# Query pass of a two-layer kernel: the output projection and the router's columns as one 136-column product, the logits read before the residual's addition

## The reference

```python
# third block, per token (q is already in its second-order form)
out = einsum(q, kv_state) / maximum(einsum(q, k_sum), 1e-5)     # 8 heads of 16
y   = out.reshape(b, n, 128) @ w_out
x   = x + layernorm(y)
# fourth block
flat = layernorm(x)
probs = softmax(flat @ Wr)            # 8 experts, the 2 best are chosen
output = sum over the chosen e of weight_e * ((silu(flat @ Wg[e]) * (flat @ Wu[e])) @ Wd[e])
x = x + layernorm(output)
```

## Time and profile before

| | |
|---|---|
| median of 3 runs | 718.79 us |
| lowest and highest run | 717.28 and 718.93 us |
| span of the profiled execution, first to last instruction | 713.3 us |
| mean granted TensorE clock over the span | 0.847 of 2.4 GHz |
| TensorE busy | 518.2 us (73%) |
| VectorE busy | 426.9 us (60%) |
| ScalarE busy | 332.8 us (47%) |

### The profile page before, as it was taken

One profiled execution on the slowest core, in us unless ns is written; L12 is line 12 of the kernel. 1 busy time (PEld: TensorE's weight loads), 2 busy tenths in 40 slices (PEclk: granted clock), 3 DMA queues, 4 the chain that ended last, 5 costly groups with the idle time before them and its releaser, 6 DMA issues.

```text
span 713.3 us, 13599 instructions
## 1 busy us (share of the span) xinstructions
PE 518.2 (73%) x3894; PEld 382.3 (54%) x3896; DVE 426.9 (60%) x1784; ACT 332.8 (47%) x690; POOL 313.0 (44%) x329
## 2 busy tenths in 40 slices
PE   1769610378777508877899997149999999999925
PEld 1457100245544303433334444149999999999921
DVE  4789668835322238898426878883545545455447
ACT  3815510044323115454357663165666666666616
POOL 3514300067878723243001112016777667767535
PEclk9966755569978758899999998559999999999976
DMA  7401272012323350100000100021111111111155
GB/s 189 130 0 56 69 291 123 6 38 41 45 43 43 34 173 28 31 15 1 2 0 16 31 27 20 15 24 42 50 48 49 46 47 48 48 44 49 38 202 167
DMA packets 47736, 42.23 MB, mean 59 GB/s; under 512 B 15346, under 2 KB 41835, under 8 KB 47179
## 3 DMA queue, kind: packets, MB, share of 16 engines
q1 hardware_dynamic: 35770, 25.48, 11.4%
q0 software_dynamic: 10816, 15.82, 10.6%
q10 hardware_dynamic: 1104, 0.39, 0.2%
HBM read 26.23 MB, written 15.30 MB: 58 GB/s over the span
## 4 chain that ended last, share of the span: by engine, by line
PE 45%; DVE 27%; issue 11%; POOL 6%; ACT 5%; DMA 4%; ACTq 1%; DVEq 0%; POOLq 0%; SPq 0%
PE bank L1886 18%; PE bank L1907 9%; DVE st L1259 3%; POOL sum_dram L673 3%; PE bank L1695 2%; PE bank L1740 2%; PE bank L1730 2%; DVE mv L1264 2%; POOL arena L661 2%; DVE st L989 2%; ACT arena L913 1%; POOL rstd L687 1%; PE bank L1796 1%; DVE hit L1103 1%; PE bank L1896 1%
## 5 line engine op out<-in xcount | busy, mean ns | idle before, releaser
L1886 PE MATMUL bank<-arena 128*128 128x128 f32 x1136 | 140.1, 277 | 0.4 <-ACT arena L964 0.4
L1886 PEld LDWEIGHTS bank<-arena 128*128 128x128 f32 x1136 | 133.9, 194 | 0.7 <-ACT arena L964 0.7
L687 POOL TENSOR_TENSOR rstd<-ve,mhalf 128x4 f32<-128x4 f32 x40 | 48.7, 1217 | 167.7 <-DVE ve L1267 121.7
L1519 DVE TENSOR_TENSOR arena<-arena,bank 128x512 f32<-128x512 f32 x71 | 48.8, 688 | 81.4 <-PE bank L1886 81.4
L741 POOL DMA_INDIRECT y_dram<-arena,sidx x71 | 69.9, 985 | 44.4 <-DVE arena L1524 41.1
L950 ACT ACTIVATE arena<-wgu 128x1024 f32 x71 | 75.0, 1057 | 26.5 <-PE bank L1886 26.2
L733 POOL DMA_INDIRECT arena<-x3row_dram,gidx x71 | 68.8, 969 | 36.5 <-issue 20.7
L1907 PE MATMUL bank<-w,arena 128*128 x568 | 75.1, 275 | 0.0
L1907 PEld LDWEIGHTS bank<-w,arena 128*128 128x128 f32 x568 | 69.1, 192 | 0.2 <-issue 0.2
L956 ACT ACTIVATE arena<-bank 128x512 f32<-128x512 f32 x71 | 42.4, 597 | 42.7 <-PE bank L1886 42.7
L673 POOL DMA_INDIRECT sum_dram<-arena,idx x32 | 50.7, 1585 | 15.2 <-issue 7.6
(11 more groups left out here) (326 smaller groups left out, 1049.0 us busy)
## 6 DMA issues: line engine op xcount, KB each, us to landing
wgu<-in_wgu SPq DMA_DIRECT2D x1, 4096.0 KB, 12.2
wgu<-y_dram SPq DMA_DIRECT2D x8, 512.0 KB, 6.7
X<-in_x SPq DMA_DIRECT2D x8, 256.0 KB, 5.6
sum_dram<-zero POOLq DMA_DIRECT2D x8, 256.0 KB, 4.2
x1row_dram<-row SPq DMA_DIRECT2D x8, 256.0 KB, 2.4
w<-in_w SPq DMA_DIRECT2D x1, 2048.0 KB, 17.4
acc<-sum_dram SPq DMA_DIRECT2D x8, 256.0 KB, 2.9
w<-in_wd SPq DMA_DIRECT2D x1, 2048.0 KB, 10.2
```

Of the source, the lines that this page charges most:

```text
L687: nc.gpsimd.tensor_tensor(out, ve[:, u], mhalf[:, 0:J], ALU.pow).then_inc(done, 1)
L1519: nc.vector.tensor_tensor(gl[:, m.pair], sgl[:, m.pair], bank[3 + m.pair][:], ALU.mult).then_inc(f_gated, 1)
L1886: last = nc.tensor.matmul(bank[first + m.pair][:, h * P:(h + 1) * P], wnow[:, m.pair, at_:at_ + P], xrT[:, m.ring], start=True, stop=True)
```

## The change

Projection and logits of a tile become one product of 136 columns: the 8 columns of `w_out @ centred Wr` are copied behind the 128 of `wo`, and the result goes to `y_lg`, four tiles of 136 columns that begin 136 columns ahead of the boundary between banks 6 and 7 (tile 0 at the end of bank 6, tiles 1 to 3 in bank 7). VectorE reads the scaled logits out of it, goes on to `mix` without waiting for them, and adds them into `lg` only afterwards. The signal `q_lgc`, for which the first four of the transposes into bank 6 wait, now comes from the first of the four residual products. For the last group nothing stands between the scaled logits and their addition.

```diff
+YW = D + E1
-        bank = [ctx.enter_context(nc.psum_tensor(f"bank{i}", [P, 512], F32)) for i in range(8)]
+        bank = [ctx.enter_context(nc.psum_tensor(f"bank{i}", [P, 512], F32)) for i in range(6)]
+        last_two = ctx.enter_context(nc.psum_tensor("bank67", [P, 1024], F32))
+        bank += [last_two[:, 0:512], last_two[:, 512:1024]]
+        y_lg = last_two[:, 512 - YW:512 + 3 * YW].rearrange("p (j n) -> p j n", j=J)
-        wo = sb("wo", [P, P])
+        wo = sb("wo", [P, YW])
-        wo_wr = sb("wo_wr", [P, E1])
-            nc.scalar.activation(wo_wr[:], bank[0][:, E1:2 * E1], ACT.Copy).then_inc(r_wr, 1)
+            nc.scalar.activation(wo[:, P:], bank[0][:, E1:2 * E1], ACT.Copy).then_inc(r_wr, 1)
             def add_logits(m):
                 ts = slice(J * m.place, J * m.place + J)
-                nc.vector.tensor_tensor(tmp[:, 0:J], bank[6][:, 0:J * E1].rearrange("p (j e) -> p j e", j=J),
-                                        rstd[:, m.b].unsqueeze(2).to_broadcast([P, J, E1]), ALU.mult).then_inc(q_lgc, 1)
-                dve.wait_ge(q_lgc, LEAD + m.n + 1)
+                ch.mark(nc.vector.tensor_tensor(tmp[:, 0:J], y_lg[:, :, D:], rstd[:, m.b].unsqueeze(2).to_broadcast([P, J, E1]),
+                                                ALU.mult))
+                if m.n < GR - 1:
+                    mix(m)
+                ch.wait()
                 do(nc.vector.tensor_tensor(lg[:, ts], lg[:, ts], tmp[:, 0:J], ALU.add))
             def mix(m):
                 for j in range(J):
                     xc = xl[:, m.place, j]
-                    last = nc.vector.scalar_tensor_tensor(xc, bank[7][:, j * P:(j + 1) * P], rstd[:, m.b, j:j + 1], xc,
-                                                          ALU.mult, ALU.add)
+                    last = nc.vector.scalar_tensor_tensor(xc, y_lg[:, j, 0:D], rstd[:, m.b, j:j + 1], xc, ALU.mult, ALU.add)
+                    if j == 0:
+                        last.then_inc(q_lgc, 1)
                 last.then_inc(q_x3, 1)
-                    stats1(lambda j: bank[7][:, j * P:(j + 1) * P], m.b, q_yvar)
+                    stats1(lambda j: y_lg[:, j, 0:D], m.b, q_yvar)
                 if m:
                     dve.wait_ge(q_yrstd, LEAD + m.n + 1)
                     add_logits(m)
-                if m and m.n < GR - 1:
-                    mix(m)
                 if m:
                     pe.wait_ge(q_ot, LEAD + m.n + 1)
                     for j in range(J):
-                        nc.tensor.matmul(bank[7][:, j * P:(j + 1) * P], oT[:, j * P:(j + 1) * P], wo[:], start=True, stop=True)
-                        last = nc.tensor.matmul(bank[6][:, j * E1:(j + 1) * E1], oT[:, j * P:(j + 1) * P], wo_wr[:], start=True,
-                                                stop=True)
+                        last = nc.tensor.matmul(y_lg[:, j], oT[:, j * P:(j + 1) * P], wo[:], start=True, stop=True)
                     last.then_inc(q_y, 1)
```

More of the change, by code:

```diff
@@ L346, in program @@
         r_wr = sem("r_router_centred")
-        q_lgc = sem("q_logits_copied")
+        q_lgc = sem("q_first_tile_added")
         r_choices = sem("r_choices")
@@ L538, in _ @@
         def _(sp):
-            tiles = dict(wqkv=wqkv, gamma=gamma, wo=wo, wr=wr, wo_t=wo_t, mask_head=mask_head, sums_of=sums_of, pairs_of=pairs_of,
+            tiles = dict(wqkv=wqkv, gamma=gamma, wo=wo[:, 0:P], wr=wr, wo_t=wo_t, mask_head=mask_head, sums_of=sums_of, pairs_of=pairs_of,
                          one_row=one_row, form_main=form_main, form_rest=form_rest, form_pair=form_pair, form_one=form_one,
```

## The result

| | before | changed |
|---|---|---|
| median of the first set of runs (4 each) | 718.86 us | 710.03 us |
| lowest and highest of them | 717.28 and 719.98 | 709.06 and 712.28 |
| ratio of the first set, 95% interval | | 0.9894 (0.9865 to 0.9923) |
| span of the profiled execution | 713.3 us | 708.4 us |
| all runs of either kernel in this study | 718.5 median of 85 (715.67 to 724.32) | 713.8 median of 22 (709.06 to 717.32) |

Yet the two spans differ by 4.9, as forecast (708.2, measured 708.4).

What follows compares the result with a forecast made beforehand. TensorE's ring of 10.84 us a turn, and VectorE behind a choice, were taken to bound the query pass; 4.07 gained plus 1.04 in turn 9 makes 5.1, so 718.79 - 5.1 = 713.7 us, range 711.5 to 717.0.

Steps and rivals of the forecast that it cites:

- The ring through TensorE: Query pass: projection, state products, second rises, their squares, next rises, projection set the turn's 10.84 us; shorter projection gains 0.81.
- the low bound: Projection: a pass of 136 columns takes 0.116 us if the weight load limits, a gain of 0.86 a turn.
- Rival B: Projection: no overlap, each pass pays its 0.105 load first; 0.07 a turn, some 0.3 in all, 718.5 us; chance 0.12.
- the order: VectorE: residual products ahead of the logits' addition, net 0.04 to 0.13 us a turn, taken as 0.08.
- its signal and the reading across two banks: Query pass: the later signal to TensorE is covered by 0.5 us or more, and reading logits over two banks costs nothing.
- One unbroken 10.84: VectorE in turns behind a choice: no slack from one projection's statistics to the next, 10.84 us.
- The leg from the statistics of turn 6 to the next rises: Query pass: 4.53 us by ScalarE, 4.56 by VectorE, instead of 5.07, so it gains 0.51.
- its 1.04: Turn 9: the half-clock projection gains 1.7 us, of which VectorE, which had waited for it, can use 1.04.
- Rival C: Query pass: VectorE and ScalarE keep more, the 0.51 and 1.04 gains fail, 3.6 us left, 715.2; chance 0.09.
- D: Query pass: TensorE idles more, its clock falls a turn earlier, turn 7 slows by some 9 us, 722.7; chance 0.07.
- what lies around it (718.79 - 713.3 = 5.5 to the median of the runs): Whole kernel: the 5.5 us between the profiled span and the runs' median, taken as unchanged.
- the clock's rise in the experts' loop: Range term: the moment the clock rises there, a run of 16 passes taking 3.55 or 2.01 us, 1.5 either way.

Runs made afterwards that it cites:

- the later rows: Changed kernel with ScalarE making the rows of group m-2 instead of m-1 in turn m: 715.39 us median of 12, query pass 79.30 against 79.33.
- idle products: Twelve unread 128x128 bf16 matmuls per group added in the key pass of both kernels: kernel before 714.4 us, changed kernel 710.2, medians of both sets.
- The later sets: Changed kernel run again twice with no edit: 714.51 us median of 9 (ratio 0.9931) and 714.77 median of 9 (ratio 0.9942).

## Why the prediction was right and wrong

**The query pass: right in its mechanism, with sizes that were off and made up for each other.** The ring through TensorE held; turns 2 to 4 are 10.1 long. A projection gained 0.75 instead of 0.81. The passes were cheaper than I took, 0.116 instead of 0.123, the low bound; what stands around the eight of them is (1.13 - 8 x 0.116) = 0.20, where I carried over the 0.09 of the kernel before. The 0.116 of the earlier trace rows was itself a little high: its passes start 0.112 apart, and the rest is the ends of the run. Rival B is excluded: 0.116 has no room for a 0.105 load in front, and the loads' row lies under the passes. By the rule of the Trainium skill ("TensorE: Matmul & The Clock Gate", Part 3, The mechanism) that a weight load overlaps only where row groups differ (the section also names loads into a background weight buffer), the projection would have stayed near 1.8; the trace doesn't agree with that rule.

On VectorE the residual products came 0.34 earlier and the addition cost 0.22, so the order gives 0.14 a turn where I took 0.08, a little over the 0.13 that I had as the most. That its signal and the reading across two banks cost nothing was right. "One unbroken 10.84" behind a choice was a wrong reading. VectorE had a gap there, and waited for the state products:

```profile
406.37 0.69 DVE L1420 COPY arena<-bank 128x512 f32<-128x512 f32 x1 [0.44 <-PE bank L1831]
```

With the shorter projection this wait is gone, but the scaled logits still come 2.69 behind the statistics (404.43 to 407.12, 412.86 to 415.55), now behind a wait of 0.59 for `rstd`, which in the kernel before was ready just then as well (406.07, 1.01 long). So this stretch was as long as I had it, for another reason. From the statistics of turn 5 to those of turn 6 are 10.64 (402.22 to 412.86) instead of 10.84, a gain of 0.20 where I had 0.08. In the sum that makes up for the projections: the statistics of turn 6 gain 2.56 where I had 2.59. (By the 0.81 a turn, the 3.8 beside it should be 4.05; nothing hangs on it.)

The leg from the statistics of turn 6 to the next rises took 4.56 (412.86 to 417.42), the number given, but by luck: the residual products started 0.12 earlier than I took, and from there to the rises were 1.76 instead of 1.64. ScalarE's way is as long, as the later rows showed, though not through its squares, which end at 417.18; it goes through the copy, the head products that wait for it, and the turning back. Turn 9 gave its 1.04 and more: its passes start 0.227 apart at the lower clock, near the 0.22 that I took. Rival C, which took these two gains away, didn't come, and neither did D: the clock was 1.00 to the same turn. So 5.09 against 5.1 is the right mechanism, and luck in the last digits: errors of 0.1 to 0.2 cancelled.

**The time: the step that failed is the one from the span to the median, and with it the range.** I took "what lies around it (718.79 - 713.3 = 5.5 to the median of the runs)" as unchanged. What lies around the span is 1.8 to 2.0 in every run. The other 3.7 were the distance of the profiled execution from its own median, and such a distance isn't carried over to another kernel: the changed kernel's profiled execution took 710.23, 1.8 above its span and next to the median of its set. The 713.7 came out right for many runs (713.8) only because their medians differ by about what the query pass gained (718.5 and 713.8, 4.7 apart; 4.4 and 5.1 in the sets with idle products). With 1.9 around the span of 708.2 I would have forecast 710.1, which the first set gave and the later ones didn't.

What made the measured 710.03 leave the range is the term for the runs' spread, 0.8 either way from three runs, with 1.5 for the clock's rise in the experts' loop. Simply added, the two would have put the lower end at 711.0, which isn't low enough either. Single runs of one kernel spread over 8 us. The experts' loop and what follows it differ by 2.0 between the profiles, within what I gave it. The larger part sits in the key pass, for which I had no term: it takes 102.9 to 107.6 us in the profiles without idle products, with a clock between 0.74 and 1.00 in a stretch. The span of 713.3 beside a median of 718.79 was on the page, and a key pass with a clock of 0.80 to 1.00 and a wait of about 2 us in most groups could have been seen in its trace.

**Open.** That the clock in the key pass causes about half of the spread is shown by the idle products; the rest isn't explained. Why all four runs of the first set fell at or below 712.28, where 2 of the 18 later ones did, isn't settled. By chance alone it would be rare: six of the 22 runs are that low, and four drawn from them at random would all be among these six about once in 500 times (an estimate that takes the runs as independent). The later sets ran on three chips; on which the first one ran isn't on record, so the chip may have a part in it. The stretch ahead of the key pass differs by up to 4.6 us between the profiles (its first product starts at 266.3 to 270.9); that wasn't followed up.

## What to carry to other kernels

Two products with the same weights and different right-hand sides are one product's weight loads too many: when the second has 8 columns, its passes cost what the loads cost (0.112 each, the same as passes of 128), and joining it gave back 0.75 of 1.88 us. Follow a gain on a ring through the turns, engine by engine: here the way through VectorE's statistics, GpSimd's `rstd` and VectorE's residual products became the longest in the turns behind a choice and took part of the gain, and an order of its own work that had been worth 0.16 us alone became worth 0.6.

Before a span is turned into a forecast of the time, find what lies around the span and how far the profiled execution lies from the median: these are two numbers. A stage with short regular waits of TensorE may run at another clock in each execution; here, filling the waits with idle products took about half of the spread away and 4 us of the time.

## What the runs showed of the hardware

Weight loads lie under the passes ahead of them, with all 128 rows in use: each float32 pass on 128x128 weights has a load of its own, which the profile shows as 0.19 us long, and yet a tile of the kernel before (two passes of 128 columns and two of 8) took 0.45, 0.112 a pass, and passes of 136 columns start 0.116 apart. At full clock a pass of 8 columns thus cost as much as one of 128: what its load costs.

In the key pass TensorE waits 1.2 to 2.6 us for VectorE in most groups. TensorE's clock fell to the lower level, 1.2 GHz, several times there (twice in the first profile of the changed kernel, six times in the second), at other moments in each execution of one kernel (clock of the stretch 302 to 320: 1.00 and 0.82 in these two). With 0.83 us of products that nobody reads put ahead of that wait, it stayed at 2.4 GHz from 284 to about 348 us in all four profiles, though up to 1.9 us of the wait were still idle. Behind the last of these products it fell once, for about 6 us, ahead of the first projection.
